# Three attentions and two feed-forwards on one core: cross values and one hidden layer in single-pass products, one weighing per pair of heads moved into the next pair's scores

## What is computed

```python
# block 0: cross-attention, 16 heads of 8, then a feed-forward
q, k, v = x @ Wq + bq, xf @ Wk + bk, xf @ Wv + bv
out = softmax(q * 8**-0.5 @ k.T) @ v @ Wo + bo
out = out + gelu(layernorm(out) @ W1 + b1) @ W2 + b2
x = x + out
# block 1: 16 heads of 64
x = attn(ln1(x), ln1(x), Wq1, Wk1, Wv1, Wo1, bo1) + x     # self-attention, 512 keys
x = attn(ln2(x), context, Wq2, Wk2, Wv2, Wo2, bo2) + x    # cross-attention, 154 keys
a, gate = split(ln3(x) @ Wp + bp)
x = a * gelu(gate) @ Wf + bf + x
```

## Time and profile before

| | |
|---|---|
| median of 3 runs | 459.2 us (458.36 to 459.84) |
| profiled execution, its own time | 462.21 us |
| its span | 460.4 us |
| TensorE matmul busy | 443.2 us, 96% of the span |
| VectorE, ScalarE, POOL busy | 277.1, 238.9, 214.5 us |
| mean granted clock of TensorE | 0.993 of 2.4 GHz |

### The profile page before, as it was taken

The page is one execution under the profiler, slowest core; times in us unless marked ns, Lnnn a source line. Parts: engine busy times, 40 slices in busy tenths (PEclk is TensorE's granted clock), DMA queues, the critical chain, the costliest instruction groups (busy, mean ns, idle before and its releaser), DMA issues.

```text
span 460.4 us, 7023 instructions
## 1 busy us (share of the span) xinstructions
PE 443.2 (96%) x2758; PEld 263.4 (57%) x2758; DVE 277.1 (60%) x511; ACT 238.9 (52%) x324; POOL 214.5 (47%) x186
## 2 busy tenths in 40 slices
PE   7999999989999999999999999999999999999896
PEld 3654665555655656655545765545575454754696
DVE  1766737576863576467656848447735577553753
ACT  2855465455557366555445526456326665237633
POOL 5488101026884796444566636873326444255010
PEclk9999899899999999999999999999999999999999
DMA  8600000000000100000001010020001000000000
GB/s 251 210 1 2 1 1 0 1 0 1 0 1 1 36 1 0 0 1 1 1 1 46 2 34 1 2 68 1 0 5 44 0 2 2 0 1 1 0 18 30
DMA packets 7985, 8.89 MB, mean 19 GB/s; under 512 B 561, under 2 KB 6129, under 8 KB 7953
## 3 DMA queue, kind: packets, MB, share of 16 engines
q1 hardware_dynamic: 7952, 8.45, 6.0%
HBM read 7.92 MB, written 0.52 MB: 18 GB/s over the span
## 4 chain that ended last, share of the span: by engine, by line
PE 86%; DVE 6%; ACT 4%; issue 2%; DMA 1%; SPq 0%
PE PV L780 18%; PE ST L749 14%; PE M L722 7%; PE ST L751 5%; PE M L828 5%; PE ST L688 5%; PE ST L650 4%; PE DEN L795 3%; ACT PT L1353 2%; PE ST L704 2%; PE ST L668 2%; PE ST L544 2%; PE ST L691 2%; PE M L870 2%; PE ST L366 1%
## 5 line engine op out<-in xcount | busy, mean ns | idle before, releaser
L1196 POOL TENSOR_TENSOR psums<-PT 128x1024 f32<-128x1024 f32 (+1 forms) x32 | 76.1, 2379 | 137.2 <-ACT PT L1353 137.1
L1353 ACT ACTIVATE PT<-ST 128x1024 f32<-128x1024 f32 (+1 forms) x96 | 98.0, 1024 | 39.6 <-PE ST L751 37.9
L1698 DVE TENSOR_REDUCE maxw<-M 128x1 f32<-128x512 f32 x128 | 83.6, 687 | 37.2 <-PE M L722 36.7
L749 PE MATMUL ST<-R 64*128 64x512 f32 (+1 forms) x576 | 105.4, 405 | 0.0
L780 PE MATMUL PV<-PT,V 128*64 128x512 f32 (+1 forms) x384 | 89.5, 601 | 0.0
L1200 POOL TENSOR_TENSOR psums<-psums,PT 128x1024 f32<-128x1024 f32 x32 | 75.9, 2373 | 2.5
L722 PE MATMUL M<-R 64*128 64x512 f32 (+1 forms) x256 | 72.0, 363 | 1.9 <-DVE maxw L1698 0.8
L749 PEld LDWEIGHTS ST<-R 64*128 64x128 f32 (+1 forms) x576 | 57.8, 171 | 14.2 <-ACT PT L1353 8.0
L722 PEld LDWEIGHTS M<-R 64*128 64x128 f32 x256 | 37.2, 185 | 38.1 <-issue 27.1
L780 PEld LDWEIGHTS PV<-PT,V 128*64 128x64 f32 (+1 forms) x384 | 24.7, 136 | 53.9 <-issue 51.5
L1361 ACT ACTIVATE AT<-PV 128x512 f32<-128x512 f32 x32 | 19.1, 598 | 62.5 <-PE PV L780 62.5
(11 more groups left out here) (257 smaller groups left out, 677.0 us busy)
## 6 DMA issues: line engine op xcount, KB each, us to landing
Wo<-in_wo SPq DMA_DIRECT2D x2, 512.0 KB, 6.4
xnT<-in_xT SPq DMA_DIRECT2D x2, 256.0 KB, 3.4
psums<-in_sel SPq DMA_DIRECT2D x1, 512.0 KB, 5.2
X<-in_x SPq DMA_DIRECT2D x1, 512.0 KB, 6.5
w<-in_w SPq DMA_DIRECT2D x2, 256.0 KB, 6.8
PT<-in_wq SPq DMA_DIRECT2D x1, 512.0 KB, 7.8
PT<-in_wk SPq DMA_DIRECT2D x1, 512.0 KB, 8.1
PT<-in_wv SPq DMA_DIRECT2D x1, 512.0 KB, 7.8
```

Source lines behind the costliest of these rows:

```text
L749: return pe.matmul(u[0:ph.KC, h, :], R[head(h), g % 3, part_k, 1, k], R[head(h), g % 3, part_q, 0, :], start=(n == 0), stop=False)
L1196: ins = pool.tensor_tensor(s, p[:, 0], p[:, 1], ALU.add)
L1353: act.activation(PT1[0:ph.KC, g % 2, c], bank(("st", g, c))[0:ph.KC, :, :], ACT.Exp, scale=HD ** -0.5).then_inc(ph.exp, 1)
L1698: ins = dve.tensor_reduce(maxw[:, g % 2, 0, at:at + 1], m[:, :], AX, ALU.max, negate=True)
```

## The change

It has five parts.

1. `late_weighing`: for pairs 0 to 14 the last weighing (unit 3) leaves the block at the end of the pair and is issued behind the second unit of the next pair's scores. ScalarE copies PV of that pair behind the third exponential of the next pair instead of ahead of the first.
2. Values of the cross-attention (pairs 8 to 11): three single-pass products on split context (`ctx2`) and split weights (`Wv`) take the place of one float32 product. POOL splits the context in pair 6; ScalarE and VectorE split the weights at the end of pair 7, when `Wv` is free.
3. `hidden(1)`: the same for W1 (split by POOL after pair 0's first sum) and the normed rows of batch 1 (ScalarE writes them also as float32r, VectorE subtracts in `trailing_first` at the end of pair 2). Its first half goes behind the projection of pair 3, its second half between that pair's first and second weighing. In pair 3 ScalarE's gelus go behind `leading(5)`, and VectorE's `trailing(5)` goes ahead of `maxima_rows(4)`.
4. Head: the transposes `to_queries0(1, 0)` go from ahead of `turn0(7)` to behind `scores_max(0, 1)`; one dummy product more stands ahead of `back0(0)`.
5. Beside the scores of pair 0 the first maxima of pair 1 stand at steps 3 and 4 of the first unit instead of 0 and 3.

```diff
@@ -80,6 +80,7 @@
         work = sb("work", [P, 2, N])
+        operand = sb("operand", [P, 2, FF], F32R)
@@ -97,6 +98,7 @@
         Wv2 = w12[0:C, :]
+        ctx2 = operand[0:C, :, 0:B * S]
@@ -190,6 +192,10 @@
+
+        def late_weighing(g):
+
+            return 0 <= g < NPAIR - 1
@@ -220,8 +226,11 @@
         var_done = [sem(f"var_done{i}") for i in range(4)]
-        split_w = {k: sem(f"split_{k}") for k in ("q1", "k1", "v1", "q2", "wp")}
-        high_w = {k: sem(f"high_{k}") for k in ("q2", "wp")}
+        split_w = {k: sem(f"split_{k}") for k in ("q1", "k1", "v1", "v2", "q2", "wp")}
+        high_w = {k: sem(f"high_{k}") for k in ("v2", "q2", "wp")}
+        w1_split = sem("w1_split")
+        ctx_split = sem("ctx_split")
+        xfirst_done = sem("xfirst_done")
@@ -353,6 +362,13 @@
+
+            def three(dst, stationary, moving):
...
+
+                for n, (v, w) in enumerate(((0, 0), (1, 0), (0, 1))):
+                    ins = pe.matmul(dst, stationary[v], moving[w], start=(n == 0), stop=(n == 2))
+                return ins
@@ -533,16 +549,24 @@
-            def hidden(b):
-
-                loaded("w1")
-                pe.wait_ge(xn_done[0], b + 1)
-                for n in (2 * b, 2 * b + 1):
+            def hidden(b, *halves):
+
+                if b == 0:
+                    loaded("w1")
+                    pe.wait_ge(xn_done[0], 1)
+                else:
+                    pe.wait_ge(w1_split, 1)
+                    pe.wait_ge(xfirst_done, 1)
+                for n in (2 * b + k for k in halves or (0, 1)):
...
                         m = 2 * (n % 2) + mm
-                        pe.matmul(u[:, mm, :], w1[:, m * P:(m + 1) * P], xnT[:, b * N:(b + 1) * N],
-                                  start=True, stop=True).then_inc(w1_done, 1)
+                        k, x = slice(m * P, (m + 1) * P), slice(b * N, (b + 1) * N)
+                        if b == 0:
+                            ins = pe.matmul(u[:, mm, :], w1[:, k], xnT[:, x], start=True, stop=True)
+                        else:
+                            ins = three(u[:, mm, :], (operand[:, 0, k], operand[:, 1, k]), (xh[:, x], xl[:, x]))
+                        ins.then_inc(w1_done, 1)
@@ -612,6 +636,7 @@
             maxima0(5, 2, 3)
+            hold(1, DEN)
@@ -643,13 +668,6 @@
-            def three(dst, stationary, moving):
...
-
-                for n, (v, w) in enumerate(((0, 0), (1, 0), (0, 1))):
-                    ins = pe.matmul(dst, stationary[v], moving[w], start=(n == 0), stop=(n == 2))
-                return ins
@@ -657,6 +675,9 @@
                         pe.wait_ge(xl_done[0], t // TB + 1)
+                    else:
+                        pe.wait_ge(ctx_split, 1)
+                        pe.wait_ge(split_w["v2"], 1)
@@ -665,7 +686,7 @@
                     else:
-                        ins = pe.matmul(u[0:r, v, :], ctxT[:, k], Wv2[:, c], start=True, stop=True)
+                        ins = three(u[0:r, v, :], (ctx2[:, 0, k], ctx2[:, 1, k]), (Wv[0:C, 0, c], Wv[0:C, 1, c]))
@@ -907,7 +928,6 @@
                 values(0, 0, 1)
-                to_queries0(1, 0)
@@ -915,6 +935,7 @@
                 scores_max(0, 1)
+                to_queries0(1, 0)
@@ -937,19 +958,19 @@
                     beside = {0: (0, (0, 0)), 2: (1, (0, 0))}
+                elif g == 0:
+                    beside = {0: (0, (3, 4)), 1: (1, (1, 3)), 2: (2, (2, 4)), 3: (3, (2, 4))}
...
                     scores(g, c, *beside.get(c, ()))
+                    if c == 1 and late_weighing(g - 1):
+                        weigh(g - 1, TB - 1)
...
-                if g == 3:
-                    hidden(1)
...
                     n, t = VALUES[g]
-                    if n == 1:
-                        loaded("wv2")
@@ -987,12 +1008,16 @@
                         project(g + 2)
+                    if g == 3:
+                        hidden(1, 0)
...
                         denominators(g - 1)
-                    for c in range(pair(g)[0].units):
+                    for c in range(pair(g)[0].units - late_weighing(g)):
                         weigh(g, c)
+                        if g == 3 and c == 0:
+                            hidden(1, 1)
@@ -1142,6 +1167,15 @@
+            def split_operand(dst, whole, done):
+
+                if done is w1_split:
+                    pool.wait_ge(ld["w1"], 16)
+                else:
+                    pool.wait_ge(w1_done, 8)
+                link(pool.tensor_copy(dst[:, 0, :], whole))
+                pool.tensor_tensor(dst[:, 1, :], whole, dst[:, 0, :].bitcast(F32), ALU.subtract).then_inc(done, 1)
@@ -1183,6 +1217,8 @@
                     add_bias(1, "bo1", 1)
+                if g == 6:
+                    split_operand(ctx2, ctxT[:, 0:B * S], ctx_split)
@@ -1199,6 +1235,8 @@
                 ins.then_inc(ph.sum, 1)
+                if g == 0:
+                    split_operand(operand, w1, w1_split)
@@ -1318,6 +1356,8 @@
                 k = slice(b * N, (b + 1) * N)
+                if n == 0 and b == 1:
+                    act.activation(xh[:, k], turned, ACT.Identity, scale=cols[:, g:g + 1], bias=cols[:, c:c + 1])
@@ -1383,23 +1423,25 @@
                         scale_features(2, 1)
-                    if g >= 1 and g != 22:
+                    if g >= 1 and g != 22 and not late_weighing(g - 1):
...
                         exponentials(g, c)
+                        if c == 2 and late_weighing(g - 1):
+                            weighted(g - 1)
...
                         weighted(g - 1)
-                    if g == 3:
-                        act.preload_act_table_set("gelu_and_others")
-                        gelus(1)
...
                         leading(g + 2)
+                    if g == 3:
+                        act.preload_act_table_set("gelu_and_others")
+                        gelus(1)
@@ -1412,6 +1454,8 @@
                         inverse_guess(g // 8 - 1)
+                    if g == 7:
+                        leading_weights("v2", Wv[0:C], Wv2)
@@ -1446,8 +1490,8 @@
-                act.wait_ge(ld["wq2" if key == "q2" else "wp"], 16)
-                act.wait_ge(*((v_done[0], NT) if key == "q2" else (self_att.proj, NPAIR)))
+                act.wait_ge(ld["w" + key if key != "wp" else key], 16)
+                act.wait_ge(*{"v2": (v_done[0], NT), "q2": (v_done[1], TB), "wp": (self_att.proj, NPAIR)}[key])
@@ -1670,6 +1714,12 @@
+            def trailing_first():
+
+                dve.wait_ge(xn_done[0], B)
+                dve.tensor_tensor(xl[:, N:2 * N], xnT[:, N:2 * N], xh[:, N:2 * N].bitcast(F32),
+                                  ALU.subtract).then_inc(xfirst_done, 1)
@@ -1773,9 +1823,11 @@
                         trailing_weights("wp", Wk, wp)
+                    if g == 3:
+                        trailing(5)
...
                         maxima_rows(g + 1)
-                    if g + 2 < NG:
+                    if g + 2 < NG and g != 3:
@@ -1783,8 +1835,12 @@
                         second_out(1)
+                    if g == 2:
+                        trailing_first()
...
                         trailing_features(1, 1)
+                    if g == 7:
+                        trailing_weights("v2", Wv[0:C], Wv2)
```

## The result

The changed kernel takes 461.34 us (median of 14, 460.68 to 462.54), the kernel before 459.13 us (14 executions, 457.88 to 460.68). The ratio is 1.0049, 95% interval 1.0038 to 1.0061: slower by half a per cent, 2.2 us. The forecast was 461.8 in 455.8 to 464.0.

What follows compares the result with a forecast made beforehand. TensorE's own queue was taken as the bound, 86% of the span. The terms 3.5 + 2.35 - 1.2 - 0.5 - 0.4 - 1.4 + 0.3 gave +2.65, so 461.8 us by the median, range 455.8 to 464.0.

Steps and rivals of the forecast that it cites:

- Late weighing, +0.25 a pair: Last weighing inside the next scores: the way in and out costs 0.25 us a pair, +3.5 over pairs 1 to 14.
- Cover taken from VectorE, +2.35: Scores start 0.85 us sooner, so TensorE waits for VectorE: +0.7, +0.6, +0.2, +0.85 in pairs 14, 9, 2, 6.
- Single passes, -1.2 and -0.5: Single-pass products save 1.2 us in cross values of pairs 8 to 11 and 0.5 in batch 1's feed-forward.
- part 6: Two new VectorE subtractions, behind pairs 2 and 7, stall TensorE some 0.1 and 0.2 us: +0.3 (0 to 2).
- Head, -0.4 and -1.4: Head: transposes moved into TensorE's idle place save 0.4 us; 2.4 GHz kept near 86 us saves 1.4.
- the 1.4 for the clock: Head: with less idle ahead of 86.3 us TensorE keeps 2.4 GHz there, -1.4 us (0 to -2.6).
- Rival A: Head: transposes don't raise the clock, the dip at 86.3 stays, the 1.4 is lost: 463.2 us, chance 0.17.
- Two subtractions, +0.3: New VectorE subtractions with both inputs in SBUF, behind pairs 2 and 7: +0.3 us of stall (0 to 2).
- part 1: Last weighing inside the next scores, pairs 1 to 15: +0.25 us a pair, +3.5 in pairs 1 to 14.
- Rival B: Weighing inserted in the scores is free, gap under 1.1 us or stage under 6.2: 456.0 us, chance 0.30.
- Rival C: Scores and head: insertion costs only +0.15 a pair and both clock dips go: 459.2 us, no change, chance 0.20.

Runs made afterwards that it cites:

- e1: The changed kernel with the last weighing back in its own pair's block, everything else kept: 456.95 us, ratio to before 0.9953.
- e2: The kernel before with only the last weighing moved into the next pair's scores: 465.35 us, ratio 1.0129.
- e10: The changed kernel with two weighing steps moved into the next scores, one behind the first unit, one behind the second: 464.37 us, ratio to before 1.0111.
- e5: The changed kernel with the last weighing moved only for pairs 1, 5 and 8, into the scores of pairs 2, 6 and 9: 460.36 us, ratio to before 1.0009.
- e6: The changed kernel with the moved weighing behind the first unit of the next scores instead of the second: 458.36 us, ratio to before 0.9975.
- e4: The kernel before with only the single-pass cross values and hidden layer of batch 1: 458.68 us, ratio 0.9982.
- e3: The kernel before with only the head's edits (moved transposes, one more dummy product, later first maxima of pair 1): 459.28 us, ratio 0.9993.
- e8: The kernel before with only the single-pass parts and the head's moved transposes: 457.02 us, ratio 0.9963.
- e11: The changed kernel with the moved weighing behind the third unit of the next scores instead of the second: 459.86 us, ratio to before 1.0024.
- e12: A repeat of e1, the changed kernel without late weighings: 456.68 us, ratio to before 0.9940.
- e9: The changed kernel with only one late weighing, that of pair 14 in pair 15's scores: 456.53 us, ratio to before 0.9942.

## Why the prediction was right, and where only its sum was

The time forecast, 461.8, was missed by 0.5 us; the terms did less well than that.

1. *Late weighing, +0.25 a pair*: right, measured 0.22 with 1.33 us between units two and three (forecast 1.35), 3.1 in 14 pairs; e1 and e2 show it by leaving the weighing out and by moving it alone, e10 by doubling. Pair 15 was forecast at 0 and gained 0.1: its stage is 5.83 us against 5.12 + 0.85. I had not asked what the place does. The 0.22 is the price behind unit two; behind unit one or three it is 0.11.
2. *Cover taken from VectorE, +2.35*: right mechanism, shown by e5 and e6. Pair 6 lost 0.84 (3.65 less 2.64, less the 0.17 that its stage of 5.51 had lost before), forecast 0.85; pair 9 0.64, forecast 0.6; pair 2 0.24, forecast 0.2. The sign of a period 0.8 us longer came true for pair 6 (1.04) and failed for pair 14 (0.21, as in a plain pair). The mis-sized term is pair 14: 0 in place of 0.7. I took the subtraction of 2.26 us as a length, but its end hangs on POOL's add. The change moved that add too: it ended at 283.17, 0.11 ahead of the first score, where it had ended 0.09 behind it. Sum 1.7.
3. and 4. *Single passes, -1.2 and -0.5*: measured -1.3 and -0.5. With the 0 of part 6 that is the 1.8 of e4's distance. For the hidden layer I had read 3.54 us to the next start where the earlier trace rows and the product behind give 3.64 (137.27 to 140.91); the two halves with their way took 3.14 in place of 3.08, so the difference came out.
5. *Head, -0.4 and -1.4*: **this step failed.** For the transposes I read the two idle pieces at 84.8 and 85.8 as what they could fill, but not what stood behind their old place. A wait for VectorE already covered them there, which no idle bracket shows, since TensorE was working. And the 1.4 for the clock, about right for the one profiled execution (28.77 against 27.3 us up to the first weighing), was taken off an execution that had the low stretch, and then carried over to the median. In 47 of 75 executions of the kernel before there is no such stretch to win back. e3 gives the sum of both terms: 0.9993 (0.9982 to 1.0004), at most 0.8 us. Rival A's claim on transposes was not settled: e8, which moves only them, differs from e4 by counts of 5 and 8 in 12. The Trainium skill, TensorE: Matmul & The Clock Gate, "Part 4: PE-mode transpose", states that transposes don't count as busy for the clock in the way products do; that is neither shown nor refuted here.
6. *Two subtractions, +0.3*: 0. The one behind pair 2 waited for POOL's running add (1.83 us) and was still done at 129.25, 0.47 ahead of VectorE's next work; the one behind pair 7 took 1.22 with POOL idle. The wait was there, the price for it wasn't, since VectorE had that much time.

So the sum of +2.65 came out near the measured +2.2 in part by luck: -1.8 of gains that weren't there stood against costs of pairs 14 and 15, of part 1 and of part 6 that were put too high by 1.5 (0.7 + 0.1 + 0.4 + 0.3). By the profiles the change costs 2.84 us (207.92 less 205.08), by the medians 2.2. Low stretches in some executions of the kernel before make up 0.2 to 0.4 of that difference in its three series (the median of all against that of the others); the rest isn't explained. Rival A's dip at 86 is gone from the profile, but no run shows that the edits did it. Rival B fell by its own mark: 1.33 us, not under 1.1, and a stage of 6.42, not under 6.2. Rival C needed 0.15 a pair; behind unit two it was 0.22, and only the places behind unit one or three come near (e6, e11).

## What to carry to other kernels

Before a step is moved into another row of work, look at what waits ahead of the new place and behind the old one: a step behind the point where the other engine is late hides nothing, and one ahead of it makes up for its way only in the pairs that wait (pair 6 of e6 costs nothing more); in the others it still costs 0.11 us here. The fastest versions left the weighing in its own block (e1, e12) or moved it only where no full-size maxima stand (e9). A term read off one profiled execution, above all one of the clock, holds only as often as that stretch occurs among the timed executions, so compare the means of their granted clocks before taking it. When an instruction's length varies from 1.2 to 2.7 us at one shape, look for the end that it waits for on another engine and move that, not the length.

## What was new of the hardware

- VectorE's subtraction with both inputs in SBUF (128x512) ended 0.54 to 0.56 us behind the POOL add under which it began, 53 times out of 53, whatever its start: 1.2 to 2.8 us long, against 0.69 with POOL idle.
- An insertion of full products into row-packed ones costs 0.11 us behind one or three of four units and 0.22 behind two; the inserted four records take 1.01 us instead of 0.85.
- Low stretches of the clock (granted 0.50, the 1.2 GHz level) came and went between executions of one kernel. In the profiles they lasted 3.41 us each (from 48.65 and 86.20 before, from 437.58 in e2) and cost 1.5 and 1.7 us where it could be told. Their place isn't fixed in the program: e2 differs from before only in pairs 0 to 15, and there the stretch came in block 1's last part.
